# First attention of a four-layer kernel: key factors folded into the queries, a row term added by VectorE, normalisation on GpSimd

## The chip, the cores and the metric

The kernel runs on one core of one Trainium2 chip. One launch computes four layers, of which the change touches the first. The metric is the device time of the launch in microseconds, lower is better. Before the change the median of three runs is 1697.05 us (1696.94 to 1702.69).

## What is computed

The first layer's attention has 16 heads of width 64 over 8 sequences of 256 tokens, each token 128 wide. z is the layer-normalised input. It passes a projection to 64 and then one to 16 heads of 64, with biases:

```python
    q = z @ wq @ fcq_w + fcq_b
    k = z @ wk @ fck_w + fck_b
    v = z @ wv @ fcv_w + fcv_b
    ...
    scores = jnp.einsum('bihd,bjhd->bhij', q, k) / scale
    attn = jax.nn.softmax(scores, axis=-1)
    out = jnp.einsum('bhij,bjhd->bihd', attn, v)
    out = out.reshape(b, n, N_HEAD * D_V)
    return out @ fco_w + fco_b
```

`scale` is 8. The rest of the reference (a routed light and heavy attention, two more attention layers with expert layers, a state space layer) is not touched.

## The kernel before

The first layer's two attention parts are one stage, `layer0_stage`, a software pipeline over units. A unit is a pair of heads of one sequence: 8 sequences times 8 pairs are the 64 "main" units (numbers 0 to 63), and 48 "light" and "heavy" units of the routed attention follow (64 to 111). Each engine has its own program, and each program runs one loop over steps u:

- TensorE, in this order: `scores(u)` (L538), the early jobs of the step (`pair` for unit u + 2, L471), `turn(u - 2)` (transposes of the probabilities, L549), `add_to_output(u - 4)` (L588), `weigh_values(u - 3)` (L572), the late jobs. `scores(u)` waits until two of the four exponentials of unit u - 1 are done, because three PSUM banks are shared. `turn(u)` waits for all four normalised pieces of its unit.
- VectorE: `negmax(u)` (L835, one reduction for each head), the early jobs' copies (L789, queries and keys with their bias), `add_output` once in 8 steps (L763), `normalise(u - 1)` (L855 reciprocal, then four L861 multiplications of 128x256), late jobs, and one iteration of the routing's descent (L191, L196, L186) in steps 6 to 55.
- ScalarE: `exponentials(u)` (L671, four of 128x256, with their sums), `save_turned(u - 2)` (L682), `save_out(u - 3)` (L687), the jobs that `by_act` names, and the descent's exponential and logarithm.
- GpSimd: three memsets, scalings of weights (L391, L394), the output bias (L401), 32 row scalings (L410), and later 32 comparisons for the choice of rows (L418, L420). In the main units it has no part in the loop.

Jobs are listed in `layer0_jobs`: those in `before` run ahead of unit 0, the others are put early or late in a step, share PSUM bank 7, and each waits until the job before it has been copied out. `values` (L496) and, in some steps, `norm_turn` (L461) are late jobs. The loads are issued by SyncE in the order `first_loads`, `fold_loads`, the other chunks of x, `main_loads`, `more_loads`.

Of the kernel before, what the change touches and what calls it, by code (L numbers as in the profile page):

```python
# [22 lines left out]
P = 128  # L23
# [200 lines left out]
def layer0_jobs(units):  # L224
# [18 lines left out]
    for g in range(1, GROUPS):  # L243
        first = [n for n, unit in enumerate(units) if unit[0] == g][0]
        if g < SEQS:
            late[first - 5].append(("values", g, 0))
            continue
# [11 lines left out]
def layer0_stage(nc, k, w, loads):  # L259
# [11 lines left out]

    def job_bank(job):

        return k.psum[(7, 6, 5, 4, 3, 2, 7, 6, 5)[number[job]] if number[job] < len(before) else JB]
# [4 lines left out]
    def by_act(job):  # L279

        what, g, i = job
        return what in ("x_turn", "fused", "norm_turn", "gather", "null_probs", "heavy_out") or (what == "values" and is_ffn(g) and i % 2 == 1)
# [48 lines left out]
    def weights_of(g, p):  # L331

        weights = w.qkv_l if is_ffn(g) else w.fused
        return weights[:, 0, P * p:P * (p + 1)], weights[:, 1, P * p:P * (p + 1)]
# [11 lines left out]
    with signals(nc, "x_loaded_0", "x_loaded_1", "x_loaded_2", "x_loaded_3", "first_loaded", "fold_loaded", "main_loaded", "weights_loaded", "variance_ready", "rstd_ready", "x_normed",  # L346
                 "moments_ready", "scales_ready", "zeroed", "scaled", "mask_cast", "null_weighted", "bias_summed", "bias_added", "rows_normed",
# [11 lines left out]
        with nc.Block() as block:  # L359

            @block.sync
            def _(sp):
# [6 lines left out]
                for c in range(1, CHUNKS):  # L369
                    sp.dma_start(k.x[:, CT * c:CT * (c + 1), :], x[:, CT * c:CT * (c + 1), :]).then_inc(x_loaded[c], 16)  # L370
                for dst, src in main_loads:
                    sp.dma_start(dst, src).then_inc(s.main_loaded, 16)
# [13 lines left out]
            def _(pool):  # L386
# [3 lines left out]
                pool.wait_ge(s.main_loaded, 16 * len(main_loads))  # L390
                nc.gpsimd.tensor_scalar(w.qkbias[:, 0, :], w.qkbias[:, 0, :], HD ** -0.5, None, ALU.mult).then_inc(s.scaled, 1)  # L391
                pool.wait_ge(s.weights_loaded, 16 * len(more_loads))
                for weights in (w.qkv_h, w.qkv_l):
                    nc.gpsimd.tensor_scalar(weights[:, 0, :], weights[:, 0, :], HD ** -0.5, None, ALU.mult).then_inc(s.scaled, 1)  # L394
                pool.wait_ge(s.scaled, 2)
                nc.gpsimd.tensor_tensor(w.null_product, w.qkv_h[:, 0, :], w.null_row, ALU.mult).then_inc(s.null_weighted, 1)
                nc.gpsimd.tensor_copy(k.window_rows[:, :], k.window_f32[:, 0:P]).then_inc(s.mask_cast, 1)
                nc.gpsimd.tensor_copy(k.window_cols[:, :], k.window_f32[:, P:P + 2 * SEQ]).then_inc(s.mask_cast, 1)
                pool.wait_ge(s.bias_summed, 1)
                pool.wait_ge(s.x_normed, TILES)  # L400
                nc.gpsimd.tensor_tensor(k.x[:, :, :], k.x[:, :, :], w.obias[:, :].unsqueeze(1).to_broadcast([P, TILES, P]), ALU.add)\  # L401
                    .then_inc(s.bias_added, 1)
                pool.wait_ge(s.scales_ready, 1)
                for q in range(SEQS):
                    if q >= 2:
                        wait_made(pool, ("norm_turn", q - 2, 0))
                    for half in range(2):
                        for t in range(SUB):
                            n = SUB * q + t
# [14 lines left out]
            def _(pe):  # L424
                def do(job):
# [5 lines left out]
                    elif n >= 6:  # L431
                        wait_saved(pe, before[n - 6])
# [2407 lines left out]
```

## Time and profile before

| | before |
|---|---|
| median of 3 runs | 1697.05 us |
| the profiled execution's own time | 1693.32 us |
| its span, first to last instruction | 1690.8 us |
| TensorE busy | 1511.7 us (89%) |
| VectorE busy | 1115.5 us (66%) |
| ScalarE busy | 955.8 us (57%) |
| GpSimd busy | 412.8 us (24%) |
| main units: first and last `scores` start | 18.8 us, 326.9 us |

Busy shares are means over all four layers. For this change the stretch of the main units counts, and there the distance between two starts of L538 is the length of a step. A wait in a row is written in brackets, with what ended it.

### The profile page before, as it was taken

Reading aid. Unit: us, or ns where it says so; the run is one execution under the profiler, and the core shown is the slowest. Engines: PE = TensorE matmul, PEld = TensorE weight load, DVE = VectorE, ACT = ScalarE, POOL = GpSimd, SP = SyncE. Lnnn points to the kernel's source line nnn. Section 1 sums busy time; section 2 is a strip of 40 time slices with the busy share of each in tenths; the row PEclk is TensorE's granted clock in tenths of the full one; section 3 lists DMA queues with packets and bytes.
Section 4 is the critical chain, followed back from the end, with each engine's and each line's share of the span. In section 5 each row is a group of like instructions: output and inputs, shape, how many; then the busy total and the mean of one; then the engine's idle time right before and its main releaser. Section 6 shows DMA issues by size and latency. Waiting matters only on the chain. (4 is left out here: it accounts for less than half of the span.)

```text
span 1690.8 us, 30916 instructions
## 1 busy us (share of the span) xinstructions
PE 1511.7 (89%) x10652; PEld 1055.9 (62%) x10652; DVE 1115.5 (66%) x2845; ACT 955.8 (57%) x2523; POOL 412.8 (24%) x429
## 2 busy tenths in 40 slices
PE   7999999998999998999999895889889876999976
PEld 4677777666666666677787763555557633555643
DVE  6788899875666664565454345787633287899964
ACT  3788888655555553544445342234344348878945
POOL 2211000200010001002220152513534402888820
PEclk9999999999999997999999997999999977999999
DMA  8000000000000003000000022200012121333300
GB/s 273 1 2 1 2 2 7 20 1 1 2 1 1 1 1 117 1 1 14 17 17 27 21 72 86 94 1 8 25 51 61 47 70 36 90 85 87 92 14 26
DMA packets 45702, 62.50 MB, mean 37 GB/s; under 512 B 7640, under 2 KB 32160, under 8 KB 44736
## 3 DMA queue, kind: packets, MB, share of 16 engines
q1 hardware_dynamic: 41008, 51.14, 10.4%
q0 software_dynamic: 4544, 9.38, 1.5%
q8 instruction: 91, 1.49, 0.4%
q14 instruction: 59, 0.48, 0.1%
HBM read 49.94 MB, written 15.75 MB: 39 GB/s over the span
## 5 line engine op out<-in xcount | busy, mean ns | idle before, releaser
L671 ACT ACTIVATE probs<-psum_all,pair_negmax 128x256 f32<-128x256 f32 x448 | 206.0, 472 | 153.1 <-DVE pair_negmax L835 103.4
L2267 POOL TENSOR_TENSOR weighted<-state,c_all 128x512 f32<-128x512 f32 x128 | 163.6, 1298 | 78.6 <-DVE state L2277 64.9
L835 DVE TENSOR_REDUCE pair_negmax<-psum_all 128x2 f32<-128x512 f32 x192 | 123.7, 686 | 71.2 <-PE psum_all L538 71.1
L2277 DVE TENSOR_TENSOR_SCAN state<-decay,psum_all 128x512 f32<-128x512 f32 x128 | 148.9, 1199 | 14.3 <-PE psum_all L2195 11.5
L861 DVE TENSOR_SCALAR probs<-probs,pair_recip 128x256 f32<-128x256 f32 x448 | 129.6, 353 | 3.9
L538 PE MATMUL psum_all<-keys,queryT 64*128 64x256 f32 x896 | 127.6, 405 | 2.1 <-DVE values L814 2.0
L682 ACT ACTIVATE probsT<-psum_all 128x512 f32<-128x512 f32 x224 | 122.4, 611 | 0.3 <-PE psum_all L549 0.3
L2205 PE MATMUL psum_all<-weighted,ident 128*128 128x512 f32 x256 | 121.7, 600 | 0.0
L549 PE MATMUL psum_all<-ident,probs 128*128 128x128 f32 x896 | 116.5, 273 | 0.1
L549 PEld LDWEIGHTS psum_all<-ident,probs 128*128 128x128 f32 x896 | 105.1, 141 | 12.5 <-issue 1.2
L1904 POOL DMA_INDIRECT found<-values,dest x78 | 74.7, 957 | 155.7 <-ACT values L1897 140.1
L538 PEld LDWEIGHTS psum_all<-keys,queryT 64*128 64x128 f32 x896 | 82.0, 191 | 37.9 <-issue 28.1
L572 PE MATMUL psum_all<-probsT,values 128*64 128x256 f32 x768 | 104.1, 392 | 0.0
L1366 ACT ACTIVATE keys<-psum_all 128x1024 f32<-128x1024 f32 x64 | 62.0, 1021 | 66.2 <-PE psum_all L1322 66.2
L1627 PE MATMUL psum_all<-values 128*128 128x65 f32 x768 | 92.8, 271 | 0.0
L2254 ACT ACTIVATE decay<-dt,a_neg 128x510 f32<-128x510 f32 x128 | 87.3, 711 | 8.7 <-DVE state L2277 7.2
L2195 PEld LDWEIGHTS psum_all<-ident,parts 128*128 128x128 f32 x512 | 60.9, 144 | 48.9 <-issue 26.6
L671 ACT ACTIVATION_READ_ACCUMULATOR probs<-psum_all,pair_negmax 128x1 f32 x448 | 90.9, 203 | 0.0
L1627 PEld LDWEIGHTS psum_all<-values 128*128 128x128 f32 x768 | 90.9, 192 | 0.0
L418 POOL TENSOR_SCALAR chosen_in<-slot_row,rank,norm_scale 128x128 f32<-128x128 f32 x16 | 12.7, 792 | 313.2 <-PE psum_all L478 166.5
L1439 DVE TENSOR_REDUCE queryT<-psum_all 128x4 f32<-128x1024 f32 x64 | 77.5, 1220 | 15.1 <-PE psum_all L1312 15.1
L1935 DVE COPY values<-psum_all 128x256 f32<-128x256 f32 (+1 forms) x78 | 43.3, 555 | 62.0 <-PE psum_all L1857 61.9
(381 smaller groups left out, 3265.1 us busy)
## 6 DMA issues: line engine op xcount, KB each, us to landing
c_all<-c_rows SPq DMA_DIRECT2D x64, 256.0 KB, 3.3
slots<-slot_fill_dram SPq DMA_DIRECT2D x2, 2535.0 KB, 14.6
ring<-slots SPq DMA_DIRECT2D x18, 260.0 KB, 3.0
keys<-found SPq DMA_DIRECT2D x16, 256.0 KB, 4.6
up<-up_dram SPq DMA_DIRECT2D x1, 2048.0 KB, 7.9
down<-down_dram SPq DMA_DIRECT2D x1, 2048.0 KB, 12.3
up<-up_dram SPq DMA_DIRECT2D x1, 1408.0 KB, 6.1
found<-values,dest POOLq DMA_INDIRECT x78, 2.2
```

The source lines that it names most:

```text
L538: last = nc.tensor.matmul(k.psum[score_bank(u, j)][:, SEQ * t:SEQ * (t + 1)], k.queryT[rows, p, at:at + P], k.keysT[rows, p, :], start=not ...
L549: last = nc.tensor.transpose(k.psum[TA + j][:, SEQ * kt + P * t:SEQ * kt + P * (t + 1)], k.probs[:, 2 * (u % PAIR_BUF) + j, t, P * kt:P * ...
L572: last = nc.tensor.matmul(k.psum[OB][HD * j:HD * (j + 1), 0:SEQ], value(g, 2 * i + j, kt), probsT[:, j, kt, :], start=(kt == 0), stop=(kt ...
L671: nc.scalar.activation(k.probs[:, 2 * (u % PAIR_BUF) + j, t, :], k.psum[score_bank(u, j)][:, SEQ * t:SEQ * (t + 1)], ACT.Exp, bias=k.pair_ ...
L682: nc.scalar.activation(k.probsT[:, 2 * (u % PAIR_TBUF) + j, :, :].rearrange("p a n -> p (a n)"), k.psum[TA + j][:, :], ACT.Copy)\
L835: nc.vector.reduce_max(k.pair_negmax[:, u % 2, SUB * j:SUB * (j + 1)], src, AXX, negate=True).then_inc(s.negmax_ready, 1)
L861: nc.vector.tensor_scalar(piece, piece, k.pair_recip[:, u % 2, i:i + 1], None, ALU.mult).then_inc(s.probs_normed, 1)
L1627: last = nc.tensor.matmul(ob[:, 2 * V1 * t + V1 * j:2 * V1 * t + V1 * (j + 1)], kernel[:, at:at + P], w.values1[:, q % 2, kt, h, :], start ...
L2205: nc.tensor.matmul(k.psum[acc(q, m)][:, :], k.ident[:, :], w.weighted[:, u % RING, :], start=(n == 0), stop=(n == L3_N - 1)).then_inc(s.su ...
L2254: nc.scalar.activation(w.decay[:, u % L3_RING, :, 1:], w.dt[:, m, CHUNK * q:CHUNK * (q + 1)].rearrange("p (b n) -> p b n", n=SEQ)[:, :, 1: ...
L2267: nc.gpsimd.tensor_tensor(w.weighted[:, u % RING, :], w.state[:, u % RING, :], w.c_all[:, u // L3_DC % C_RING, :], ALU.mult)\
L2277: nc.vector.tensor_tensor_scan(w.state[:, u % RING, :], w.decay[:, u % L3_RING, :, :].rearrange("p b n -> p (b n)"), k.psum[u % PARTS_RING ...
```

## The change

- Keys are no longer made for each pair. `wk` is applied once a sequence (job `keys`, 128 columns that hold the 64 key features twice, into `k.yT`), and the per-head key matrix is multiplied into the query weights ahead of unit 0 (`query_turn`, `fused`). So `pair` makes only the query, and VectorE copies only that.
- The biases are folded too: job `biases` (24 small products) gives a bias of the folded query, and a column per head that is appended to the value weights, so that `values` also yields a term for each row and head (`row_term`). That term is constant along a score row.
- VectorE, after both reductions of a main unit, computes `row_max` = negmax - term and then `pair_shift` = `row_max` + term, in two instructions of 128x4 on both heads, each behind a semaphore wait. `exponentials` of a main unit wait for `shift_ready` instead of each head's `negmax_ready`.
- `normalise(u)` of a main unit ends on VectorE with the reciprocal; the four multiplications go to GpSimd, one after the other, and `turn` waits for `pool_normed`.
- `save_out` of a main unit moves from ScalarE (step u + 3) to VectorE, first thing in step u + 4.
- The rest of GpSimd's work is cut into slices between the normalisations: weight scalings at step 3, null weights and mask casts at step 4, one row scaling a step from step 4, the output bias by sequence at steps 9 to 16, two choices at steps 60 and 62, six after the last main unit.
- Ahead of unit 0 VectorE's statistics of the x chunks are interleaved with the jobs; `fold_turn`, `fold`, `bias` move one step later each; `fold_loads` grows from two loads to seven, and the value part of `fc` and then `wo` come after the x chunks.

```diff
-    before += [("x_turn", 0, 0), ("fused", 0, 0), ("fused", 0, 2), ("fused", 0, 1), ("fused", 0, 3), ("fold_turn", 0, 0), ("pair", 0, 0), ("pair", 0, 1),
-               ("values", 0, 0)]
-    for step, jobs in enumerate(([("fold", 0, 0)], [("fold", 0, 1), ("x_turn", 0, 1)], [("bias", 0, 0), ("x_turn", 0, 2)], [("x_turn", 0, 3)], [("logits", 0, 0)])):
+    before += [("x_turn", 0, 0), ("query_turn", 0, 0), ("query_turn", 0, 1), ("keys", 0, 0), ("fused", 0, 0), ("biases", 0, 0), ("pair", 0, 0), ("pair", 0, 1),
+               ("values", 0, 0), ("fused", 0, 1)]
+    for step, jobs in enumerate(([("fold_turn", 0, 0)], [("fold", 0, 0), ("x_turn", 0, 1)], [("fold", 0, 1), ("x_turn", 0, 2)], [("bias", 0, 0), ("x_turn", 0, 3)],
+                                 [("logits", 0, 0)])):
...
+                def normalise(u):
+                    pool.wait_ge(s.recip_ready, u + 1)
+                    for i in range(2 * SUB):
+                        piece = k.probs[:, 2 * (u % PAIR_BUF) + i // SUB, i % SUB, :]
+                        nc.gpsimd.tensor_scalar(piece, piece, k.pair_recip[:, u % 2, i:i + 1], None, ALU.mult).then_inc(s.pool_normed, 1)
+
+                for u in range(SEQS * PAIRS + 1):
+                    if is_main(u - 1):
+                        normalise(u - 1)
+                    if u == 3:
+                        scale_weights()
+                    if u == 4:
+                        weigh_null()
+                        cast_mask()
+                    if 0 <= u - 4 < 4 * SEQS:
+                        norm_row((u - 4) // 4, (u - 4) % 4)
+                    if 0 <= u - 9 < SEQS:
+                        add_bias(u - 9)
+                    if u in (60, 62):
+                        choose((u - 60) // 2)
+                for q in range(2, SEQS):
...
+                    elif what == "query_turn":
+                        pe.wait_ge(s.fold_loaded, 16 * len(fold_loads))
+                        for j in range(4):
+                            p = 4 * i + j
+                            last = nc.tensor.matmul(jb[:, P * j:P * (j + 1)], w.fc[:, 0, P * p:P * (p + 1)], w.inT[:, 0, :], start=True, stop=True)
+                    elif what == "keys":
+                        wait_saved(pe, x_turned(g))
+                        last = nc.tensor.matmul(jb[:, 0:SEQ], w.wk[:, :], k.xnT[:, tokens(g)], start=True, stop=True)
...
                     elif what == "fused":
-                        pe.wait_ge(s.fold_loaded, 16 * len(fold_loads))
-                        last = nc.tensor.matmul(jb[:, :], w.inT[:, i // 2, :], w.fc[:, i // 2, CHUNK * (i % 2):CHUNK * (i % 2 + 1)], start=True, stop=True)
+                        wait_saved(pe, ("query_turn", 0, i))
+                        for j in range(4):
+                            p = 4 * i + j
+                            last = nc.tensor.matmul(jb[:, P * j:P * (j + 1)], w.query_turned[:, p, :], w.key_fold[:, p, :], start=True, stop=True)
+                    elif what == "biases":
+                        for n in range(2):
+                            wait_saved(pe, ("query_turn", 0, n))
+                        for p in range(PAIRS):
+                            heads = slice(2 * p, 2 * p + 2)
+                            nc.tensor.matmul(jb[:, heads], w.query_turned[:, p, :], w.kbias[:, heads], start=True, stop=True)
+                            nc.tensor.matmul(jb[:, HEADS + 2 * p:HEADS + 2 * p + 2], w.qbias[:, p:p + 1].to_broadcast([P, P]), w.kbias[:, heads], start=True, stop=True)
+                            last = nc.tensor.matmul(jb[:, 2 * HEADS + p:2 * HEADS + p + 1], w.key_fold[:, p, :], w.qbias[:, p:p + 1], start=True, stop=True)
                     elif what == "fold_turn":
...
+                            last = nc.tensor.matmul(jb[:, P * t:P * t + HD + HEADS], k.xnT[:, first:first + P], w.wv[:, :], start=True, stop=True)
...
-                    pe.wait_ge(s.probs_normed, 2 * SUB * (u + 1))
+                    mains = min(u + 1, SEQS * PAIRS)
+                    if u >= SEQS * PAIRS:
+                        pe.wait_ge(s.probs_normed, 2 * SUB * (u + 1 - SEQS * PAIRS))
+                    pe.wait_ge(s.pool_normed, 2 * SUB * mains)
...
+                        if is_main(u):
+                            act.wait_ge(s.shift_ready, u + 1)
+                        else:
+                            act.wait_ge(s.negmax_ready, 2 * u + n + 1)
+                        shift = k.pair_shift if is_main(u) else k.pair_negmax
                         for t in range(SUB):
                             i = SUB * j + t
                             nc.scalar.activation(k.probs[:, 2 * (u % PAIR_BUF) + j, t, :], k.psum[score_bank(u, j)][:, SEQ * t:SEQ * (t + 1)],
-                                                 ACT.Exp, bias=k.pair_negmax[:, u % 2, i:i + 1], accum_out=k.pair_sum[:, u % 2, i:i + 1]).then_inc(s.probs_ready, 1)
+                                                 ACT.Exp, bias=shift[:, u % 2, i:i + 1], accum_out=k.pair_sum[:, u % 2, i:i + 1]).then_inc(s.probs_ready, 1)
...
+                        row_term = w.row_term[:, g % 2, :, 2 * p:2 * p + 2].rearrange("p t j -> p j t")
+                        dve.wait_ge(s.negmax_ready, 2 * (u + 1))
+                        nc.vector.tensor_tensor(four(w.row_max[:, :]), four(k.pair_negmax[:, u % 2, :]), row_term, ALU.subtract).then_inc(s.row_max_ready, 1)
+                        dve.wait_ge(s.row_max_ready, u + 1)
+                        nc.vector.tensor_tensor(four(k.pair_shift[:, u % 2, :]), four(w.row_max[:, :]), row_term, ALU.add).then_inc(s.shift_ready, 1)
...
+                def save_out(u):
+                    dve.wait_ge(s.values_weighed, u + 1)
+                    nc.vector.tensor_copy(k.outT[:, units[u][0] % 2, out_place(u), :], k.psum[OB][:, 0:SEQ]).then_inc(s.out_saved, 1)
...
                 chunk_norm(0)
-                for c in range(1, CHUNKS):
-                    chunk_statistics(c)
+                chunk_statistics(1)
+                for job in before[:4]:
+                    do(job)
+                chunk_statistics(2)
+                do(before[5])
+                chunk_statistics(3)
                 second_scales()
-                for job in before:
+                for job in before[6:]:
                     do(job)
                 for u in steps:
+                    if is_main(u - O_AFTER):
+                        save_out(u - O_AFTER)
                     if u < U:
                         negmax(u)
                     for job in early[u]:
@@ -906,7 +1002,7 @@
                         chunk_norm(u + 1)
                     for job in late[u]:
...
+        fold_loads = [(w.inT[:, :, :], d["inT"]), (w.fc[:, 0, :], d["fc"][:, 0, :]), (w.key_fold[:, :, :], d["key_fold"]), (w.wk[:, :], d["wk0"]),
+                      (w.qbias[:, :], d["qbias"]), (w.kbias[:, :], d["kbias"]), (w.wv[:, 0:HD], d["wv0"])]
+        main_loads = [(w.wo[:, :, :], d["wo0"])]
```

## Rows read from the trace of the kernel before

**Rows 1.** Windows view of the main units: stretch, us, busy (x instructions), clock, DMA share.

```profile
60.00:180.00 120.00, 120.00 (x861) 88.75 (x859) 105.55 (x312) 103.48 (x369) 14.14 (x24) 1.00 0.01 1
```

**Rows 2.** Timeline, TensorE's weight loads over one step: start us, us, engine, line, tile, shapes.

```profile
268.45 0.73 PEld L538 LDWEIGHTS psum_all<-keys,queryT 64*128 64x128 f32 x8 [0.39 <-issue]
269.52 0.73 PEld L471 LDWEIGHTS psum_all<-xnT,fused 128*128 128x128 f32 x4 [0.33 <-issue]
270.27 1.01 PEld L549 LDWEIGHTS psum_all<-ident,probs 128*128 128x128 f32 x8
271.25 0.53 PEld L588 LDWEIGHTS psum_all<-wo_folded,outT 128*128 128x128 f32 x4
271.90 0.63 PEld L572 LDWEIGHTS psum_all<-probsT,values 128*64 128x64 f32 x8
272.91 0.52 PEld L496 LDWEIGHTS psum_all<-wv,xnT 128*128 128x128 f32 x4 [0.38 <-issue]
273.50 0.73 PEld L538 LDWEIGHTS psum_all<-keys,queryT 64*128 64x128 f32 x8
```

**Rows 3.** Timeline of all engines, the step that starts at 120.34 us.

```profile
120.34 0.73 PEld L538 LDWEIGHTS psum_all<-keys,queryT 64*128 64x128 f32 x8 [0.39 <-issue]
...
121.53 1.29 DVE L835 TENSOR_REDUCE pair_negmax<-psum_all 128x2 f32<-128x512 f32 x2 [0.28 <-PE psum_all L538]
...
122.31 0.48 ACT L671 ACTIVATE probs<-psum_all,pair_negmax 128x256 f32<-128x256 f32 x1 [0.29 <-DVE pair_negmax L835]
...
122.73 0.48 DVE L789 TENSOR_SCALAR queryT<-psum_all,qkbias 128x256 f32<-128x256 f32 x1
...
123.12 0.48 DVE L789 TENSOR_SCALAR keys<-psum_all,qkbias 128x256 f32<-128x256 f32 x1
123.13 0.20 ACT L671 ACTIVATION_READ_ACCUMULATOR probs<-psum_all,pair_negmax 128x1 f32 x1
...
123.90 0.42 DVE L763 TENSOR_TENSOR x<-x,psum_all 128x256 f32<-128x256 f32 x1 [0.30 <-PE psum_all L588]
...
124.24 0.17 DVE L855 RECIPROCAL pair_recip<-pair_sum 128x4 f32<-128x4 f32 x1
124.44 1.14 DVE L861 TENSOR_SCALAR probs<-probs,pair_recip 128x256 f32<-128x256 f32 x4
```

**Rows 4.** Timeline, TensorE's weight loads: starts of step 5 and of step 60.

```profile
55.49 0.73 PEld L538 LDWEIGHTS psum_all<-keys,queryT 64*128 64x128 f32 x8 [0.42 <-issue]
...
309.52 0.73 PEld L538 LDWEIGHTS psum_all<-keys,queryT 64*128 64x128 f32 x8 [0.38 <-issue]
```

**Rows 5.** Groups by line with shapes kept apart, GpSimd alone: xcount, busy us, mean ns, idle before.

```profile
L410 POOL TENSOR_SCALAR values<-xn,norm_scale 128x128 f32<-128x128 f32 x32 | 19.0, 606 | 106.5 <-PE psum_all L461 106.5
L1228 POOL TENSOR_SCALAR values<-queryT,head_rows 128x256 f32<-128x256 f32 x32 | 17.6, 559 | 2.4 <-POOL queryT L1223 1.8
...
L394 POOL TENSOR_SCALAR qkv_h<-qkv_h 128x512 f32<-128x512 f32 x1 | 1.6, 1565 | 11.1 <-DMA rot_sin<-rot_sin_dram 11.1
...
L391 POOL TENSOR_SCALAR qkbias<-qkbias 128x8 f32<-128x8 f32 x1 | 0.2, 250 | 11.0 <-DMA wo<-wo_dram 11.0
```

**Rows 6.** Timeline: an instruction of GpSimd that waits for one of VectorE.

```profile
40.08 0.29 DVE L805 TENSOR_TENSOR obias<-obias,psum_all 128x128 f32<-128x128 f32 x1 [0.82 <-PE psum_all L453]
...
40.45 4.54 POOL L401 TENSOR_TENSOR x<-x,obias 128x2048 f32<-128x2048 f32 x1 [10.90 <-DVE obias L805]
```

**Rows 7.** Timeline of the start, up to the first scores, and the bias job.

```profile
10.30 3.70 PE L439 MATMUL psum_all<-fc,in_T 64*128 64x512 f32 x8
...
12.98 0.84 DVE L727 BATCH_NORM_STATS2 stats<-x 128x6 f32<-128x128 f32 x4
...
15.36 0.21 DVE L752 RECIPROCAL norm_scale<-norm_scale 128x16 f32<-128x16 f32 x1
...
18.82 1.39 PEld L538 LDWEIGHTS psum_all<-keys,queryT 64*128 64x128 f32 x8 [2.15 <-DVE values L814]
...
37.02 2.05 PE L451 MATMUL psum_all<-wo,vbias 128*128 128x128 f32 x16
```

More of the change, by code:

```diff
@@ L245, in layer0_jobs @@
         if g < SEQS:
+            late[first - 6].append(("keys", g, 0))
             late[first - 5].append(("values", g, 0))
@@ L270, in layer0_stage @@
     first_loads, fold_loads, main_loads, more_loads = loads
+    OPENING = (7, 6, 5, 4, 2, 7, 6, 5, 4, 3)
     def job_bank(job):
-        return k.psum[(7, 6, 5, 4, 3, 2, 7, 6, 5)[number[job]] if number[job] < len(before) else JB]
+        return k.psum[OPENING[number[job]] if number[job] < len(before) else JB]
     def is_ffn(g):
@@ L281, in by_act, with is_main @@
         what, g, i = job
-        return what in ("x_turn", "fused", "norm_turn", "gather", "null_probs", "heavy_out") or (what == "values" and is_ffn(g) and i % 2 == 1)
+        return what in ("x_turn", "fused", "norm_turn", "gather", "null_probs", "heavy_out") or (what, i) == ("query_turn", 0) \
+            or (what == "values" and is_ffn(g) and i % 2 == 1)
+    def is_main(u):
+        return 0 <= u < U and units[u][1] == "main"
     def saved_count(job):
@@ L331, in weights_of @@
     def weights_of(g, p):
-        weights = w.qkv_l if is_ffn(g) else w.fused
-        return weights[:, 0, P * p:P * (p + 1)], weights[:, 1, P * p:P * (p + 1)]
+        cols = slice(P * p, P * (p + 1))
+        return (w.qkv_l[:, 0, cols], w.qkv_l[:, 1, cols]) if is_ffn(g) else (w.fused[:, p, :],)
     def out_weights(g, p):
@@ L412, in _, with choose @@
-                for q in range(SEQS):
+                    half, t = i // SUB, i % SUB
+                    n = SUB * q + t
+                    nc.gpsimd.tensor_scalar(w.norm_rows[q % 2][:, SUB * half + t, :], k.xn[:, n, :], w.norm_scale[:, half, n:n + 1], None, ALU.mult)\
+                        .then_inc(s.rows_normed, 1)
+                def choose(q):
                     pool.wait_ge(s.ranked, q + 1)
@@ L464, in do @@
                         if not is_ffn(g):
-                            for half in range(2):
-                                wait_saved(pe, ("fused", 0, 2 * half + i // 4))
+                            wait_saved(pe, ("fused", 0, i // 4))
                         else:
-                            pe.wait_ge(s.scaled, 3)
+                            pe.wait_ge(s.scaled, 2)
                         src = w.xlT if is_ffn(g) else k.xnT
@@ L521, in scores @@
                     wait_saved(pe, ("heavy_keys" if kind == "heavy" else "pair", g, i))
+                    if kind == "main":
+                        wait_saved(pe, ("keys", g, 0))
                     if u >= 1:
@@ L708, in _ @@
                         save_turned(u - T_AFTER)
-                    if 0 <= u - V_AFTER < U:
+                    if 0 <= u - V_AFTER < U and not is_main(u - V_AFTER):
                         save_out(u - V_AFTER)
```

118 lines of the change are left out of this document (69 added, 49 removed).

## The prediction

> **What bounds the kernel now.** I read the windows view first, since the busy shares of the page are means over four layers. In the steady part of the main units TensorE is busy for all of its 120 us at full clock, VectorE for 105.6 and ScalarE for 103.5 of them, GpSimd for 14 [rows 1]. Then the timeline of TensorE's weight loads, to see what a step is made of. From start to start, scores hold TensorE for 1.07 us, the pair job for 0.75, the transposes for 0.98, the output products for 0.65, the values for 1.01, together 4.46; a late `values` job adds 0.59 [rows 2]. No load there waits for another engine. So the steady step is TensorE's own work. Steps 5 to 60 take 309.52 - 55.49 = 254.0 us [rows 4], that is 55 x 4.46 = 245.3 and 15 late jobs (8 `norm_turn`, 7 `values`) of about 0.59. Last the timeline of all engines in one step, to see when each reaches its part [rows 3]; counted from the start of scores (120.34), the reductions start at 1.19 and last 1.29, the first exponential starts at 1.97, the fourth exponential of the previous unit has long been done, and the query copy starts at 2.39, the key copy 0.39 later.
>
> **What the change removes.** A pair job has four records of TensorE, 256 columns each; two go. Four of them take 1.0 to 1.1 us of TensorE's time, so about 0.49 a step: TensorE's own step becomes 3.97. The `keys` job gives back 0.49 once in eight steps. VectorE loses four multiplications (1.14) and a key copy (0.39) in each step [rows 3] and takes over the copy of the output (0.42, as the L763 addition of the same size) and two small instructions; with waits these come to 2 x 0.20, as the reciprocal and what waits for it are 0.20 apart [rows 3]. Its mean load falls by 0.7 a step. ScalarE loses a copy of some 0.4. Neither of the two is the limit before or after: each was busy under 90% [rows 1], and both lose work. `values` with 80 columns for 64 costs nothing beside its weight loads, which have the same number; its second VectorE instruction is behind the reciprocal, in VectorE's idle time.
>
> **First new wait: exponentials.** They wait for both reductions and two small instructions: shift ready at 1.19 + 1.29 + 0.03 + 0.20 + 0.17 = 2.88, first exponential at 2.97 for 1.97 before, one microsecond later. Two exponentials with their sums end 1.02 after the first begins (122.31 to 123.33 [rows 3]), so scores(u + 1) can start at 2.97 + 1.02 + 0.07 = 4.06. That alone would give a step of 4.06, under 4.46; it is covered as long as something else takes longer.
>
> **Second new wait: GpSimd.** This is the term that decides. The reciprocal of unit u - 1 stands in VectorE's program behind negmax(u), so behind scores(u). Counted from the start of scores(u): shift ends 2.88 (row subtraction starts at 2.51, addition at 2.71), the query copy occupies 2.82 to 3.21, the reciprocal 3.21 to 3.38, taken as 3.40. GpSimd starts 0.08 after VectorE ends (40.37 to 40.45 [rows 6]), does four pieces of P each, and I take another 0.08 to TensorE. So turn(u - 1), in step u + 1, can't start before 3.56 + 4P. Behind it in TensorE's queue stand the output products, the values and the late jobs, and then scores(u + 2): 0.98 + 0.65 + 1.01 = 2.64 [rows 2]. Hence two steps last at least 6.20 + 4P. Before, VectorE did the pieces in 1.14 instead of 4P, and this chain had room.
>
> **The price P** of one 128x256 multiplication on GpSimd is not in the trace; its neighbours are [rows 5]. L410 is the same instruction (one multiplication by a column of scalars) on 128 columns: 0.606. L394 on 512 columns, with a constant: 1.565. L391 on 8 columns: 0.250. The line from 128 to 512 columns gives 0.93 at 256, the line from 8 to 128 gives 0.99. L1228, a multiplication and an addition on 128x256, took only 0.559. Bounds 0.56 and 0.99. I take 0.90: L410 is the nearest in form, at half the size it already takes more than L1228, and 512 columns on the same line speak for a cost that grows with the columns.
>
> The Trainium skill (GPSIMD Engine Reference, section 3.1, "Elementwise — side-by-side cycle accounting") gives a best case of about 1.8 cycles an element and 769 ns for 512 elements. The trace does not agree for this form: 512 columns took 1.565 us [rows 5]. By the page's rate 256 columns would be an estimate of some 0.4 us and a little dispatch, the two steps some 8.0 us, and the change a gain; by the rows it is a loss.
>
> **The steady sum.** With P = 0.90, two steps last 9.80 and one 4.90; 55 steps 269.5. Late jobs lie between turn and the next scores, so they lengthen the chain, but only the chain of odd or of even units that they fall in. `keys` (u mod 8 = 2), `norm_turn` (0 and 4, up to 36) and the addition of the output, which stands ahead of the reciprocal in VectorE's program (u mod 8 = 3), all delay the odd chain: 7 x 0.49 + 8 x 0.59 + 7 x 0.4 = 10.9 (0.4 being what of its 0.42 and its wait is not hidden). `values` delays the even one by 4.1, which is hidden behind the other chain once they have drifted apart. Sum 280.4 for 254.0: **+26.4 us**. GpSimd has 3.6 of pieces, 0.6 of a row scaling and at steps 9 to 16 a bias slice (an eighth of L401's 4.54 [rows 6] and a fixed part, so about 0.7) in each step, 4.9 in all, just its step: +1 for that. Steps 60 to 63 have four comparisons each at 60 and 62 (128 columns, so L410's 0.61 apiece or more), which delay a normalisation by 1 to 1.5 twice; against that VectorE, which has the ranks there, is lighter. I take 0, between -4.4 (four times its 1.14) and +3.
>
> **The start.** Before, scores(0) start at 18.82 [rows 7]. After: loads for the fold are there by about 10.3, as now. Two `query_turn` jobs are 16 records at 0.128 (L451: 16 records in 2.05), to 12.4; a copy of 512 columns, some 0.7, to 13.1; `biases` is 24 products, 48 records with a weight load each, at 0.128: 6.1, to 19.2. Then VectorE has three small instructions (0.6), the statistics of the last chunk and the second scales (12.98 to 15.57: 2.6 [rows 7]), two query copies (0.8) and the values' two (0.5), to 23.7: **+5.0**. x's chunks are issued behind five more loads, which stays hidden under `biases`. In steps 1 to 3 VectorE sets the pace (normalisation, x rows, copies of the folds, in a row), and it loses 1.14 + 0.39 and gains 0.40: 1.1 a step, **-3.3**. SyncE issues `wo` and the other weights later, behind seven loads instead of two; they are first used late in steps 1 and 3, eight us and more behind the first scores, which is their cover. If it fell, a load that is late by one us would cost one us, once. Net +1.7.
>
> **Sum**: 26.4 + 1 + 0 + 1.7 = +29.1 us. The profiled execution took 1693.3 us with its 1690.8 span; that gives 1722.4. The median of the runs shown lies 3.7 higher, so 1726; I say **1725**, that is 1.6% slower.
>
> **Rivals.**
> - The forecast: TensorE waits for GpSimd in every step, +20 to +37. Chance 0.65.
> - GpSimd takes P = 0.99 or is slowed beside VectorE, the late jobs of both chains count (+4), and the start costs 4 more: 279.4 + 10.9 + 4 - 254.0 + 2.7 + 4 = +47, so 1744. For it: the 8-to-128 line. Against: it needs each term at its end. Chance for the part above +37: 0.15.
> - P is 0.64 to 0.72: the step is 4.38 to 4.54, the sum 0 to +9, so 1697 to 1706. For it: a high fixed cost in L410's 0.606. Against: 512 columns at 1.565. Chance 0.11.
> - The other side: GpSimd does this form at L1228's rate, 0.56. Two steps are 8.44, one 4.22, 55 of them 232.1; with 10.9 and 2.7 that is -8.3, and up to 4.4 less at the end: 1684 to 1689. It decides below P = 0.64, where 55T + 10.9 + 2.7 = 254. Against it: L410, half the size, is dearer. Chance 0.09.
>
> **Range and chances.** About 0.5% (8.5 us) is what a measurement can tell from no change. The range goes from P = 0.69 to nearly the second rival: 1702 to 1742. Slower by over 0.5%: 0.65 and 0.15, so 0.80; within 0.5%: most of the third, 0.12; faster: 0.08.
>
> **What would show it.** In the profile after, the windows view should show TensorE busy some 82% of the steady part, GpSimd near 75 to 90%, and L549's weight loads waiting for GpSimd, 0.5 to 1 us a step. The distance of two L538 starts should alternate between long and short with a mean near 5.1. The GpSimd group of 128x256 probabilities should have a mean near 0.90; at 0.56 the prediction falls. L671 should start 2.97 after L538. The first L538 should start near 24 us.

## The result, and the profile after

The changed kernel takes 1733.38 us (median of 4 runs, 1732.78 to 1735.2) against 1696.99 for the kernel before; the ratio is 1.0185 with a 95% interval of 1.0159 to 1.0211. By this interval it is slower by 27 to 36 us; the two medians differ by 36.4. The forecast was 1725, with a range of 1702 to 1742.

The windows view of the changed kernel, same columns and first stretch as [rows 1]:

```profile
60.00:180.00 120.00, 105.11 (x738) 71.36 (x738) 84.25 (x244) 83.38 (x304) 102.13 (x125) 1.00 0.00 1
180.00:300.00 120.00, 104.33 (x740) 71.05 (x740) 84.60 (x246) 84.51 (x314) 90.69 (x104) 1.00 0.00 1
```

TensorE, which was busy for all 120 us, now is for 105; VectorE and ScalarE fell from 105.6 and 103.5 to 84. GpSimd went from 14 to 102 and 91. No engine is full, and the kernel is slower all the same: that points to a chain from engine to engine. The view of waits from 60 to 340 us (who waited for whom, us in total, times, longest) names it:

```profile
ACT probs L740 <- DVE pair_shift L921: 70.6, 54, 4.7
POOL probs L443 <- DVE pair_recip L939: 57.6, 38, 3.3
PEld psum_all L612 <- POOL probs L443: 51.5, 43, 2.0
PE psum_all L612 <- POOL probs L443: 34.9, 35, 1.6
```

The line to read is the third: TensorE's transposes wait for GpSimd, 51.5 us in 43 waits. The timeline shows one turn of the chain, unit u's scores at 204.60; the bracket gives the wait:

```profile
204.60 0.73 PEld L598 LDWEIGHTS psum_all<-yT,queryT 64*128 64x128 f32 x8 [0.17 <-issue]
...
205.79 1.29 DVE L912 TENSOR_REDUCE pair_negmax<-psum_all 128x2 f32<-128x512 f32 x2 [1.23 <-PE psum_all L598]
...
207.11 0.16 DVE L919 TENSOR_TENSOR row_max<-pair_negmax,row_term 128x4 f32<-128x4 f32 x1
207.31 0.17 DVE L921 TENSOR_TENSOR pair_shift<-row_max,row_term 128x4 f32<-128x4 f32 x1
207.39 0.48 DVE L853 TENSOR_SCALAR queryT<-psum_all,fused_bias 128x256 f32<-128x256 f32 x1
207.57 0.47 ACT L740 ACTIVATE probs<-psum_all,pair_shift 128x256 f32<-128x256 f32 x1 [1.31 <-DVE pair_shift L921]
...
207.78 0.17 DVE L939 RECIPROCAL pair_recip<-pair_sum 128x4 f32<-128x4 f32 x1
...
208.05 3.65 POOL L443 TENSOR_SCALAR probs<-probs,pair_recip 128x256 f32<-128x256 f32 x4 [1.78 <-DVE pair_recip L939]
...
208.70 0.76 PEld L598 LDWEIGHTS psum_all<-yT,queryT 64*128 64x128 f32 x8 [0.43 <-issue]
...
211.75 0.86 PEld L612 LDWEIGHTS psum_all<-ident,probs 128*128 128x128 f32 x8 [1.65 <-POOL probs L443]
...
212.57 0.53 PEld L652 LDWEIGHTS psum_all<-wo_folded,outT 128*128 128x128 f32 x4
...
213.22 0.63 PEld L635 LDWEIGHTS psum_all<-probsT,values 128*64 128x64 f32 x8
...
214.23 0.30 PEld L483 LDWEIGHTS psum_all<-xnT,wk 128*128 128x128 f32 x2 [0.39 <-issue]
...
214.86 0.73 PEld L598 LDWEIGHTS psum_all<-yT,queryT 64*128 64x128 f32 x8 [0.33 <-issue]
```

Counted from 204.60: reductions at 1.19, shift computed by 2.88, first exponential at 2.97, reciprocal at 3.18, GpSimd's pieces from 3.45 to 7.10, transposes of that unit at 7.15, and TensorE is through with what stands behind them at 9.63 (214.23), where in this step a `keys` job comes before the scores (0.63 more). In between lies one step that nothing holds up, 4.10 long. Elsewhere the wait is shared out between the two steps, unevenly: TensorE's weight loads of a stretch without late jobs wait 0.60 us for GpSimd in one step and 1.33 in the next, and the steps are 4.44 and 5.19 long, sum 9.63:

```profile
266.12 0.73 PEld L598 LDWEIGHTS psum_all<-yT,queryT 64*128 64x128 f32 x8 [0.39 <-issue]
...
268.08 0.86 PEld L612 LDWEIGHTS psum_all<-ident,probs 128*128 128x128 f32 x8 [0.60 <-POOL probs L443]
...
270.56 0.73 PEld L598 LDWEIGHTS psum_all<-yT,queryT 64*128 64x128 f32 x8 [0.39 <-issue]
271.63 0.30 PEld L528 LDWEIGHTS psum_all<-xnT,fused 128*128 128x128 f32 x2 [0.33 <-issue]
273.26 0.85 PEld L612 LDWEIGHTS psum_all<-ident,probs 128*128 128x128 f32 x8 [1.33 <-POOL probs L443]
...
275.75 0.73 PEld L598 LDWEIGHTS psum_all<-yT,queryT 64*128 64x128 f32 x8 [0.39 <-issue]
```

GpSimd's groups in the changed kernel, for comparison with [rows 5] (xcount, busy us, mean ns, idle before):

```profile
L443 POOL TENSOR_SCALAR probs<-probs,pair_recip 128x256 f32<-128x256 f32 x256 | 233.1, 926 | 102.3 <-DVE pair_recip L939 102.3
...
L425 POOL TENSOR_SCALAR values<-xn,norm_scale 128x128 f32<-128x128 f32 x32 | 19.2, 599 | 0.0
...
L417 POOL TENSOR_TENSOR x<-x,obias 128x256 f32<-128x256 f32 x8 | 5.8, 727 | 0.0
```

The start of the changed kernel: first and last record of `biases` on TensorE, then VectorE's statistics, the last of the second scales, the query copies, and the first scores, for comparison with [rows 7]:

```profile
13.08 0.28 PE L494 MATMUL psum_all<-kbias,query_turned 128*128 128x2 f32 x2
...
18.66 0.57 PE L496 MATMUL psum_all<-qbias,key_fold 128*128 128x1 f32 x2
...
19.50 0.86 DVE L796 BATCH_NORM_STATS2 stats<-x 128x6 f32<-128x128 f32 x4
...
21.89 0.22 DVE L821 RECIPROCAL norm_scale<-norm_scale 128x16 f32<-128x16 f32 x1
22.03 0.80 DVE L853 TENSOR_SCALAR queryT<-psum_all,fused_bias 128x256 f32<-128x256 f32 x2
...
23.62 1.09 PEld L598 LDWEIGHTS psum_all<-yT,queryT 64*128 64x128 f32 x8 [0.22 <-issue]
```

The steps can be added up from the starts of scores in the traces:

| stretch | before | after | difference | forecast |
|---|---|---|---|---|
| up to scores(0) | 18.82 | 23.62 | +4.8 | +5.0 |
| steps 0 to 4 | 36.67 | 36.28 | -0.4 | -3.3 |
| steps 5 to 59 | 254.03 | 279.89 | +25.9 | +27.4 |
| steps 60 to 63 | 24.57 | 25.75 | +1.2 | 0 |
| up to scores(64) | 334.09 | 365.54 | +31.4 | +29.1 |

The two spans differ by more, 40.2 us. The other 8.8 lie behind scores(64), in code that the change leaves alone, most of it in the second attention; that is taken up with the last experiments and isn't counted as an effect of the change.

### The profile page after: what moved, and what is told of

It reads as the page before. It is cut to its first block and busy times, and to the rows that moved or that the text cites. A ratio compares the mean times of both kernels' runs of the same rounds, so it can differ in the third digit from the quotient of the medians.

```text
span 1731.0 us, 30977 instructions
## 1 busy us (share of the span) xinstructions
PE 1507.0 (87%) x10612; PEld 1036.9 (60%) x10612; DVE 1079.1 (62%) x2737; ACT 932.2 (54%) x2458; POOL 645.6 (37%) x691
## 5 line engine op out<-in xcount | busy, mean ns | idle before, releaser
L443 POOL TENSOR_SCALAR probs<-probs,pair_recip 128x256 f32<-128x256 f32 x256 | 233.1, 926 | 102.3 <-DVE pair_recip L939 102.3
L740 ACT ACTIVATE probs<-psum_all,pair_shift 128x256 f32<-128x256 f32 x256 | 117.7, 472 | 97.9 <-DVE pair_shift L921 93.6
L740 ACT ACTIVATE probs<-psum_all,pair_negmax 128x256 f32<-128x256 f32 x192 | 88.3, 472 | 106.1 <-DVE pair_negmax L912 59.9
L612 PEld LDWEIGHTS psum_all<-ident,probs 128*128 128x128 f32 x896 | 100.9, 141 | 63.0 <-POOL probs L443 55.3
L1871 POOL DMA_INDIRECT slots<-probs,slot x32 | 31.8, 994 | 197.5 <-DVE slot L1196 115.3
L2344 ACT ACTIVATE parts<-xdtT,b_cols 128x256 f32<-128x256 f32 x192 | 83.0, 497 | 1.9 <-PE psum_all L2291 1.9
L2291 PE MATMUL psum_all<-ident,parts 128*128 128x128 f32 x512 | 69.5, 279 | 16.0 <-ACT parts L2344 12.1
```

What stands on the lines that cost most here:

```text
L443: nc.gpsimd.tensor_scalar(piece, piece, k.pair_recip[:, u % 2, i:i + 1], None, ALU.mult).then_inc(s.pool_normed, 1)
L612: last = nc.tensor.transpose(k.psum[TA + j][:, SEQ * kt + P * t:SEQ * kt + P * (t + 1)], k.probs[:, 2 * (u % PAIR_BUF) + j, t, P * kt:P * ...
L740: nc.scalar.activation(k.probs[:, 2 * (u % PAIR_BUF) + j, t, :], k.psum[score_bank(u, j)][:, SEQ * t:SEQ * (t + 1)], ACT.Exp, bias=shift[: ...
L2291: last = nc.tensor.transpose(k.psum[u % PARTS_RING][:, P * j:P * (j + 1)], w.parts[:, r % 2, j, P * m:P * (m + 1)], k.ident[:, :])
```

## Experiments

Each is judged by the length of steps 5 to 59 (called S below: start of scores(60) less start of scores(5)), because that number was 254.03 in both profiles of the kernel before, and by the ratio of times with its interval.

**1. VectorE normalises again.** One part of the change is undone.

```diff
                     dve.wait_ge(s.recip_ready, u + 1)
-                    if is_main(u):
-                        return
                     for j in range(2):
...
-                    mains = min(u + 1, SEQS * PAIRS)
-                    if u >= SEQS * PAIRS:
-                        pe.wait_ge(s.probs_normed, 2 * SUB * (u + 1 - SEQS * PAIRS))
-                    pe.wait_ge(s.pool_normed, 2 * SUB * mains)
+                    pe.wait_ge(s.probs_normed, 2 * SUB * (u + 1))
```

> The changed kernel with one part undone: VectorE does the four multiplications of a main unit again, all else as changed (row term, output copy on VectorE, folded keys). Theory (TensorE waits for GpSimd in the two-step chain): the wait of the transposes is gone. VectorE then has 0.42 + 1.29 + 0.40 + 0.39 + 0.20 + 1.14 + 0.92 = 4.76 us in each step with a descent iteration and becomes the limit, so steps 5 to 60 take 262 to 270 us instead of 279.9, and the launch 1712 to 1722 us. Rival (the exponentials that start one us later set the step): no change, 279.9 us and 1733 us.

Measured: S = 262.1, 1718.15 us, ratio 1.0092 (1.0063 to 1.0122). Windows view:

```profile
60.00:180.00 120.00, 108.42 (x776) 76.51 (x774) 112.82 (x343) 86.77 (x313) 26.96 (x35) 1.00 0.01 1
180.00:300.00 120.00, 109.77 (x797) 78.79 (x794) 113.93 (x373) 92.73 (x342) 6.52 (x8) 1.00 0.00 1
```

And the start of a step without late jobs, TensorE's row of scores in the timeline from 257 to 263 us:

```profile
257.33 1.13 PE L597 MATMUL psum_all<-yT,queryT 64*128 64x256 f32 x8 [0.88 <-ACT probs L736]
```

S lies at the low edge of what was expected, but not as the expectation had it: such steps are 4.42 long, not VectorE's 4.76. VectorE is busy for 113 and 114 of 120 us, and its reductions start 1.53 us after the scores for 1.19 elsewhere. That puts the first exponential at 3.29, the end of the second with its sum at 4.31, and the next scores at 4.42; the row shows scores waiting for an exponential. So the exponentials hold these steps, pushed back by a full VectorE: what was named as the rival is half of the answer. Undoing GpSimd's part gives back 17.8 of the 25.9 us; the other 8 are this second obstacle.

**2. The reciprocal ahead of the reductions.** GpSimd still does the multiplications, at the same price; only its start moves.

```diff
                         save_out(u - O_AFTER)
+                    if is_main(u - 1):
+                        normalise(u - 1)
                     if u < U:
                         negmax(u)
...
-                    if 1 <= u <= U:
+                    if 1 <= u <= U and not is_main(u - 1):
                         normalise(u - 1)
...
+                    if is_main(u) and u >= 2:
+                        dve.wait_ge(s.pool_normed, 2 * SUB * (u - 1))
                     nc.vector.reciprocal(...)
```

(The last two lines keep the reciprocals' buffer from being written while GpSimd still reads it.)

> The changed kernel with the reciprocal of unit u - 1 moved ahead of the reductions of unit u in VectorE's program; GpSimd still normalises. Theory (the chain runs through VectorE's order: reductions, shift, query copy, reciprocal, four pieces on GpSimd, transposes): GpSimd starts 2.5 us earlier, two steps need 7.5 us, which is no longer the limit. GpSimd's own load is then the next one: 3.65 + 0.60 of a row scaling to step 35, 0.73 of bias at steps 9 to 16, so 4.3 to 5.0 us a step, later the exponentials' 4.06. Steps 5 to 60: about 243 us, the launch about 1697 us. Rival (GpSimd is simply too slow at 0.91 a piece, wherever it starts): 275 to 280 us, 1730 us.

Measured: S = 250.3 (243 was expected), 1700.52 us, ratio 0.9995 (0.9975 to 1.0016). Timeline of one step:

```profile
257.95 0.76 PEld L598 LDWEIGHTS psum_all<-yT,queryT 64*128 64x128 f32 x8 [0.44 <-issue]
...
258.78 0.18 DVE L941 RECIPROCAL pair_recip<-pair_sum 128x4 f32<-128x4 f32 x1 [0.20 <-ACT probs L740]
...
259.05 3.62 POOL L443 TENSOR_SCALAR probs<-probs,pair_recip 128x256 f32<-128x256 f32 x4 [0.50 <-DVE pair_recip L941]
...
260.93 0.47 ACT L740 ACTIVATE probs<-psum_all,pair_shift 128x256 f32<-128x256 f32 x1 [0.62 <-DVE pair_shift L921]
...
262.06 0.76 PEld L598 LDWEIGHTS psum_all<-yT,queryT 64*128 64x128 f32 x8 [0.44 <-issue]
```

From scores at 257.95 the reciprocal now is at 0.83 instead of 3.18 and GpSimd starts at 1.10. The step is 4.11, steady, with no alternation. S fell by 29.6 us while GpSimd's work is the same. So GpSimd's throughput was enough, and the loss was the length of the chain, of which the place of a 0.17 us instruction in VectorE's program is one part. GpSimd isn't what holds the step now: its four pieces fill 3.62 of 4.11. The first exponential, at 260.93, is still 2.98 behind its scores, and two must be done before the next scores; the second ends with its sum at 261.95 and the scores start at 262.06. That leads to experiment 6. Of the 7 us above the expected 243, 3 are plain steps of 4.12 for 4.06; the rest lies in steps with late jobs and was not taken apart.

**3. The same multiplication with an addition of zero.**

```diff
-nc.gpsimd.tensor_scalar(piece, piece, k.pair_recip[:, u % 2, i:i + 1], None, ALU.mult)
+nc.gpsimd.tensor_scalar(piece, piece, k.pair_recip[:, u % 2, i:i + 1], w.zero_col[:, 0:1], ALU.mult, ALU.add)
```

> The changed kernel with GpSimd's multiplication written as a multiplication and an addition of a column of zeros, the form of the masked keys of a later layer, which took 0.56 us for 128x256. Same chain. Theory (the step is (6.20 + 4P)/2): if the form brings P to 0.56, two steps are 8.44, steps 5 to 60 about 243 us, the launch about 1697 us. Rival (P hangs on the size alone and stays 0.91): no change, 279.9 and 1733 us. I hold the first for 0.6.

Measured: S = 249.75 (243 was expected), 1705.72 us, ratio 1.0018 (0.9997 to 1.0038). GpSimd's groups:

```profile
L445 POOL TENSOR_SCALAR probs<-probs,pair_recip,zero_col 128x256 f32<-128x256 f32 x256 | 145.3, 581 | 158.9 <-DVE pair_recip L941 158.9
...
L427 POOL TENSOR_SCALAR values<-xn,norm_scale 128x128 f32<-128x128 f32 x32 | 19.3, 602 | 0.0
```

The mean of one falls from 926 to 581 ns on the same data, as L1228 had it [rows 5]. So the prediction's bounds for the price, 0.56 and 0.99, were two forms of one instruction. The chain's formula, two steps = 6.20 + 4P, gives 8.52 or 4.26 a step at 0.581; the shortest steps measured 4.10 to 4.17, as in experiment 2, so the formula is a little long here too. Either repair alone reaches the same next limit, the later start of the exponentials.

The Trainium skill (GPSIMD Engine Reference, section 3.1) has a best case of about 1.8 cycles an element, 769 ns for 512. For 256 columns that makes an estimate of 0.4 us and a dispatch. The form with the addition, 0.58 measured, is nearer to it than the form with one multiplication, 0.93, which the figure does not fit.

**4. GpSimd's part alone**, in the kernel before: L861's multiplications of main units on GpSimd, its other work sliced as in the changed kernel, all else as before. The edit is the diff of `normalise`, `turn` and the GpSimd program shown with the change.

> The kernel before with one part of the change alone: GpSimd normalises the main units (with its other work cut into slices as in the changed kernel); keys, biases, output copy and start as before. Theory: reciprocal ends at 3.34 after the start of scores (reductions, two copies), so two steps need 3.34 + 0.08 + 3.65 + 0.08 + 2.64 = 9.79 us, as in the changed kernel, and the saving of TensorE's time in the changed kernel is worth nothing: steps 5 to 60 take 278 to 284 us instead of 254.0, the launch 1722 to 1730 us. Rival (the row term and the late exponentials carry most of the loss): under 1705 us.

Measured: S = 274.6, 1721.59 us, ratio 1.0112 (1.0059 to 1.0164). Windows view:

```profile
180.00:300.00 120.00, 114.50 (x800) 80.39 (x798) 79.47 (x202) 94.33 (x346) 91.83 (x104) 1.00 0.00 1
```

20.5 of the 25.9 us arise from this part alone. Steps alternate 4.48 and 5.15, two are 9.63, as in the changed kernel, although the pair job there has half the records and here all of them: the 0.43 us that the folded keys save of TensorE's time in each step (4.46 to 4.03, experiments 6 and 7) buys nothing while TensorE waits for GpSimd. S is under what was expected (278 to 284), and more by the chain than by the late jobs: two steps take 9.63 for 9.79, which is 4.4 us in 55 steps, while what comes on top of the chain is 9.8 us. The launch time lies just under its range.

**5. No row term.** The two small instructions go, and each head's exponentials wait for its own reduction. In exact arithmetic the shift is the same number.

```diff
-                    if is_main(u):
-                        ...
-                        nc.vector.tensor_tensor(four(w.row_max[:, :]), four(k.pair_negmax[:, u % 2, :]), row_term, ALU.subtract)...
-                        dve.wait_ge(s.row_max_ready, u + 1)
-                        nc.vector.tensor_tensor(four(k.pair_shift[:, u % 2, :]), four(w.row_max[:, :]), row_term, ALU.add)...
...
-                            act.wait_ge(s.shift_ready, u + 1)
+                        act.wait_ge(s.negmax_ready, 2 * u + n + 1)
```

> The changed kernel without the two small VectorE instructions of the row term (the shift is the plain negated maximum, which is what subtracting and adding the term gives but for rounding); each head's exponentials wait for its own reduction as before, one us earlier. GpSimd normalises, reciprocal in its late place. Theory (chain through reciprocal and GpSimd): the reciprocal comes 0.40 us earlier, two steps last 9.4 instead of 9.8, steps 5 to 60 take 268 to 272 us for 279.9, the launch about 1724 us. Rival (the late exponentials set the step): the whole loss goes, 254 us or less, launch under 1708 us.

Measured: S = 268.9, as forecast, 1706.98 us, ratio 1.0107 (1.0062 to 1.0151); that session's kernel before had a median of 1687.38. The launch time is 17 us under what was expected, and that lies behind the first layer: from scores(64) to the end this profile has 1349.8 us and that of the changed kernel 1365.4 (see experiment 8). The same holds of the launch times expected for experiments 6 and 7. The exponentials started a full microsecond earlier and S fell by 11.0, which is 0.40 in two steps: only what the reciprocal came earlier. In the presence of the GpSimd chain the late exponentials cost nothing of their own.

**6. Early reciprocal and no row term** (experiments 2 and 5 together).

> The early reciprocal, and in addition no row term in the shift, as in the run before in this call. Theory: with the early reciprocal the steps of 4.12 us were held by the exponentials (two of unit u must be done before the scores of u + 1); without the row term that bound falls to 3.1 and the next is GpSimd's load, 3.65 us a step and 0.60 of a row scaling to step 35, 0.73 of bias at steps 9 to 16, and TensorE's own 3.97. The shortest steps fall from 4.12 to about 3.97, steps 5 to 60 from 250.3 to about 242 us, launch about 1693 us. Rival (the 4.12 is GpSimd's or VectorE's): no change from 250.3.

Measured: S = 239.65, 1676.39 us, ratio 0.9944 (0.9927 to 0.9962). The shortest steps are 4.03. The edit also takes two instructions from VectorE, but the rows of experiment 2 show the second exponential ending 0.11 before the scores. So the 4.12 of experiments 2 and 3 was the exponentials' bound, forecast as 4.06 behind the GpSimd chain and covered by it in the changed kernel. Removing it is worth 10.7 us here.

**7. All three edits**, with the form of experiment 3, and without the products that served only the row term (`biases` 8 products for 24, `values` 64 columns for 80).

```diff
                         for p in range(PAIRS):
-                            heads = slice(2 * p, 2 * p + 2)
-                            nc.tensor.matmul(jb[:, heads], w.query_turned[:, p, :], w.kbias[:, heads], ...)
-                            nc.tensor.matmul(jb[:, HEADS + 2 * p:HEADS + 2 * p + 2], w.qbias[:, p:p + 1].to_broadcast([P, P]), w.kbias[:, heads], ...)
                             last = nc.tensor.matmul(jb[:, 2 * HEADS + p:2 * HEADS + p + 1], w.key_fold[:, p, :], w.qbias[:, p:p + 1], ...)
```

> Early reciprocal, no row term, and GpSimd's multiplication in the form with an addition of zero, at 0.56 us; the products for the row term are dropped as well (job biases 8 products for 24, values 64 columns for 80). Theory: TensorE alone sets the step, 55 x 3.97 + 15 x 0.59 + 7 x 0.49 = 231 us for steps 5 to 60; the first scores start 4 us earlier than 23.6, at 19.5. Launch 1675 to 1682 us, 1.2% under the kernel before. Rival (VectorE, which now reads and writes more of the copies, or ScalarE becomes the limit): steps of 4.1 and more, 240 us.

Measured: S = 235.8, 1666.60 us, ratio 0.9871 (0.9852 to 0.9889): faster than the kernel before by 1.3%, clear of the interval, where 1.2% was expected. The windows view shows TensorE full again:

```profile
60.00:180.00 120.00, 118.93 (x874) 85.39 (x874) 85.53 (x230) 101.29 (x372) 81.93 (x147) 1.00 0.01 1
180.00:300.00 120.00, 119.64 (x877) 85.22 (x874) 86.70 (x245) 95.81 (x353) 64.93 (x118) 1.00 0.03 10
```

S was expected at 231; a plain step is 4.03, not 3.97, which is 3.3 of the 4.8 us. It is 3.8 under experiment 6, so the cheaper form still counts there: GpSimd's busy time from 60 to 180 us is 81.9 here and 116.8 of 120 in experiment 6. The first scores start at 19.69, 3.9 earlier than in the changed kernel.

**8. The kernel before once more**, for its profile alone.

> The kernel before, unchanged, for a second profile: the stretch of the second attention (unchanged code) took 167 us in its first profile and 173 to 176 us in that of every changed kernel. If that is chance, this profile shows 173 to 176 too; if it hangs on the change, 167.

Measured: span 1688.0, S = 254.03, scores(64) at 334.31, so the first layer repeats to within 0.3 us. The stretch of the second attention (first to last start of its L1312 products, or the same line in the other kernels) took 165.8 us here. In the kernels profiled in the same session, experiments 5, 6 and 7, it took 167.1, 167.2 and 165.9, though they carry the change; in experiments 1 to 4, of an earlier session, 174.1, 176.4, 173.3 and 172.6; in the changed kernel 174.9, in the first profile of before 167.1. So the change does not force the longer stretch: three kernels that carry it show the short one. That it goes with the session fits the kernel before itself, whose medians in the two sessions were 1701.2 and 1687.4; but no profile of the kernel before was taken in a session with the long stretch, so this isn't shown in full.

**9. All of it without GpSimd**: as experiment 7, but VectorE normalises with the reciprocal in its late place.

> As the kernel with all three edits, but VectorE normalises, with the reciprocal in its late place, and GpSimd has no part in the main units: folded keys, no row term, output copy on VectorE. It tells whether GpSimd is worth using at all once its work is placed well. Theory: VectorE's order holds the step at its load, 0.42 + 1.29 + 0.39 + 0.17 + 1.14 + 0.92 = 4.35 us with a descent iteration, and copies of late jobs on top, so steps 5 to 60 take 246 to 252 us (235.8 with GpSimd, 254.0 before), launch 0.4 to 0.7% under the kernel before. Rival (VectorE has room, TensorE sets the step either way): 236 us, 1.2% under.

Measured: S = 240.1, 1689.96 us, ratio 0.9935 (0.9918 to 0.9951). Windows view:

```profile
60.00:180.00 120.00, 115.92 (x847) 82.54 (x844) 115.21 (x329) 99.08 (x355) 27.16 (x35) 1.00 0.01 1
180.00:300.00 120.00, 118.28 (x871) 84.76 (x869) 114.50 (x357) 98.76 (x354) 3.25 (x4) 1.00 0.03 10
```

S misses its range of 246 to 252 on the side of the rival: plain steps are 4.03 although VectorE is 96% busy. The sum of its durations (4.33 when added up, 4.35 in the expectation) overstates its load, for its instructions overlap: the two copies of [rows 3] last 0.48 each and start 0.39 apart. The ratio is in its range. Against experiment 1 (S = 262.1) this kernel lacks the row term and what makes it. VectorE is as full and its reductions are as late in both (about 1.55 and 1.53 after the scores), but here the first exponential starts at 2.3 and there at 3.29. With VectorE full, those two instructions, their waits and the late exponentials cost 22 us.

GpSimd, with the reciprocal early and the cheaper form, adds 4.2 us of S (240.06 against 235.84) to what folded keys without a row term bring. Up to scores(64) the two kernels are 7.4 us apart (320.66, 313.30). The two ratios differ by 0.6%, some 11 us, but the interval of each is some 3 us wide on either side, so the other 3 to 4 us can't be told from nothing.

## Why the prediction was right, point by point

- **What bounded the kernel** (TensorE in every step): right. Whatever lets TensorE work without waits gives plain steps of 4.03 (experiments 6, 7, 9), and the 0.43 us under 4.46 is what the halved pair job saves, 0.49 having been forecast.
- **The chain through GpSimd**, 6.20 + 4P for two steps: right in mechanism and size. 9.80 was forecast, 9.63 measured. The parts: reciprocal begins at 3.18 (3.21 forecast), GpSimd starts at 3.45 (3.48), its four pieces take 3.65 (3.60), handing over 0.05 (0.08), transposes to next scores 2.49 (2.64). Experiments 1, 2, 3 and 4 bear it out from four sides: other engine, other start, other price, alone.
- **The price of one piece**, 0.90: measured 0.913 back to back (3.65 for four) and 0.926 as a mean. The line through 128 and 512 columns of the same form had given 0.93. The rival at L1228's rate was real, but for another form; experiment 3 shows where it would have led.
- **Late jobs**: 10.9 and 1 for GpSimd's load were forecast. A `keys` job costs 0.63, not 0.49. With 55 x 4.815 = 264.8 for the plain chain, 15.1 remain of the measured 279.9, against 11.9. The two errors, a chain too long by 4.7 and extras too short by 3.2, nearly cancel: that S came out within 1.5 us is luck to this extent. Which late job makes up the rest of the extras was not tried.
- **Exponentials**: first one at 2.97, as forecast to the hundredth; alone a bound of 4.06, measured 4.12 (experiments 2 and 3), and 4.42 where a full VectorE pushes it back (experiment 1). That it is covered by the chain was right (experiment 5).
- **The start**: +4.8 for +5.0. The steps behind it were mis-sized: -0.4 for -3.3. One by one, steps 0 to 4 differ by -1.5, -0.6, -0.8, +2.9 and -0.4. What VectorE loses does pay: in experiment 4, which leaves jobs and keys as they were, the same five steps take 32.0 for 36.7. In the changed kernel two things take it back. One is the new `keys` job of the second sequence, in step 2: it waits for the freshly turned x and then stands ahead of the next scores. Timeline of the changed kernel:

```profile
41.86 0.60 ACT L706 ACTIVATE xnT<-psum_all 128x512 f32<-128x512 f32 x1
...
42.51 0.70 PE L483 MATMUL psum_all<-xnT,wk 128*128 128x256 f32 x2 [0.69 <-ACT xnT L706]
43.14 0.73 PEld L598 LDWEIGHTS psum_all<-yT,queryT 64*128 64x128 f32 x8 [0.33 <-issue]
```

  TensorE waits 0.7 us for ScalarE's copy and works 0.6 (42.51 to 43.14) before it comes to the next scores. The other is the bias job, which moved from step 2 to step 3. There it starts at 46.72 and TensorE's next job at 50.37, and VectorE has nothing to do beside it (idle for 3.35 us before it adds the result), where in step 2 of the kernel before it ran beside VectorE's multiplications and x rows. No run moved it back, so its share is read from the traces alone.
- **Steps 60 to 63**: +1.2 for 0, within the bounds given (the lower one, four times 1.14, is -4.6 and not -4.4, which changes nothing).
- **Level**: through the first layer the traces give +31.4 for +29.1; the ratio gives +27 to +36, the medians +36.4. Of the 8 us by which 1733 lies above 1725, only these 2.3 belong to the first layer. The later layers, put at no change, took 8.8 more in the profile.
- **The signs**: mean step 5.09 for 5.1, GpSimd busy for 85% and 76% for 75 to 90%, waits of 0.60 and 1.33, first scores at 23.6 for 24. One missed: TensorE was busy for 88% and 87% of the steady part, not 82%.

## What to carry to other kernels

Before giving a step to a slower engine, follow one item through the engines' programs and count from the event that releases it to the one that needs it: GpSimd had the throughput, 3.65 us in a step of 4.8, and still cost 18 to 21 us (experiments 1 and 4), since its start was chained behind a reduction that it did not need. Moving one reciprocal of 0.17 us ahead in its queue gave 30 us back. And here the saving on the bounding engine, half a pair job in each of 64 steps, came to light only after the chain beside it was shorter.

## What the runs showed that was not expected

- GpSimd multiplies 128x256 by a column in 0.93 us, and multiplies and adds a column of zeros in 0.58 us, the same operands otherwise. The form with more arithmetic is the faster one. Why is not known from these runs.
- VectorE at 96% busy (115.2 of 120 us) did not lengthen the plain step: 4.03 with it and with VectorE at 71% (experiments 9 and 7). With the row term behind the reductions, VectorE at 94% went with plain steps of 4.42 (experiment 1).
- In the second attention the granted clock of TensorE differed between profiles of code that is the same. In the changed kernel, the 40 us around its end show 0.83 and 0.91 of 2.4 GHz as means of 20 us, so a part of them at the lower level of 1.2 (windows view, same columns):

```profile
1220.00:1240.00 20.00, 18.36 (x219) 11.36 (x216) 13.49 (x19) 7.38 (x11) 9.82 (x13) 1.00 0.07 22
1240.00:1260.00 20.00, 14.95 (x149) 8.61 (x150) 8.00 (x11) 6.55 (x8) 11.18 (x13) 0.83 0.10 31
1260.00:1280.00 20.00, 16.15 (x190) 9.90 (x194) 8.00 (x14) 10.42 (x14) 7.91 (x9) 0.91 0.08 28
```

  The first of the three rows is the 20 us before the fall: clock 1.00, TensorE busy for 18.4 of them; then 0.83 with 15.0 busy. The first profile of before shows 1.00 in the corresponding stretch:

```profile
1200.00:1220.00 20.00, 17.43 (x210) 11.01 (x214) 12.81 (x17) 8.10 (x11) 11.12 (x15) 1.00 0.06 19
1220.00:1240.00 20.00, 15.94 (x218) 9.82 (x218) 9.19 (x15) 11.01 (x14) 12.30 (x14) 1.00 0.14 44
```

  From its first scores to the start of the last three steps the second attention takes 151.9 us in the changed kernel and 150.4 in the kernel before, and from there to its last scores 23.0 and 16.7. So 6.3 of the 7.8 us lie where the clock fell, and 1.5 ahead of it, at full clock. Whether the lower clock makes the 6.3 or comes with it, these runs don't show. No change of the first layer is known to explain them, which is the reason to compare stretches of the trace rather than spans.
